# Root term formed at the head of the second edge loop, a middle stage written out by chunk, and the last additions' places read ahead

## The reference

```
h = max(layernorm(x), 0)
msg = relu(concat(h[src], h[dst], w) @ W1 + b1) @ W2 + b2
agg = segment_max(msg, dst)            (0 where a node has no edge)
x = x + relu(concat(h, agg) @ U1 + c1) @ U2 + c2
h = max(layernorm(x), 0)
W[r] = sum over b of w_comp[r, b] * weight[b]          (8 relations, 4 bases)
x = x + relu(h @ root_weight + segment_sum((h @ W[rel])[src], dst) + bias)
```

## Time and profile before

| | us |
|---|---|
| median of 3 runs (8218.98 to 8224.45) | 8222.21 |
| the profiled execution | 8227.52 |
| its span, to which all places below refer | 8225.5 |
| GpSimd busy | 5991.5 (73%) |
| TensorE busy | 5838.0 (71%) |
| VectorE busy | 4033.0 (49%) |
| ScalarE busy | 921.0 (11%) |

### The profile page before, as it was taken

The page is one execution under the profiler, slowest core; times in us unless marked ns, Lnnn a source line. Parts: engine busy times, 40 slices in busy tenths (PEclk is TensorE's granted clock), DMA queues, the critical chain, the costliest instruction groups (busy, mean ns, idle before and its releaser), DMA issues. The chain is left out here.

```text
span 8225.5 us, 99087 instructions
## 1 busy us (share of the span) xinstructions
PE 5838.0 (71%) x23786; PEld 4086.1 (50%) x23786; DVE 4033.0 (49%) x7231; ACT 921.0 (11%) x1415; POOL 5991.5 (73%) x6283
## 2 busy tenths in 40 slices
PE   6878878878778888888766666666666666666655
PEld 5555555555555555555544444444444444444444
DVE  5555555555555555555564444444444444444443
ACT  3111111111111111111130000000000000000001
POOL 4777777777777777777627777777777777777775
PEclk8998998899999888888887777777777777777777
DMA  6333333333333333333332222222222222222223
GB/s 183 99 99 97 97 99 97 97 98 98 97 97 99 97 97 97 99 97 97 86 85 53 53 53 53 53 53 53 53 53 53 53 53 53 53 53 53 53 53 68
DMA packets 452815, 644.74 MB, mean 78 GB/s; under 512 B 156658, under 2 KB 273082, under 8 KB 452260
## 3 DMA queue, kind: packets, MB, share of 16 engines
q0 software_dynamic: 200704, 411.44, 19.9%
q1 hardware_dynamic: 239284, 226.22, 9.9%
q10 hardware_dynamic: 12768, 6.42, 0.3%
HBM read 615.44 MB, written 28.13 MB: 78 GB/s over the span
## 5 line engine op out<-in xcount | busy, mean ns | idle before, releaser
L552 POOL DMA_INDIRECT G<-p_tab,idxs x3136 | 3031.2, 967 | 970.2 <-issue 950.6
L1106 POOL DMA_INDIRECT hT<-h_tab,idxs x3136 | 2959.0, 944 | 964.1 <-issue 953.6
L671 DVE TENSOR_TENSOR_SCAN R<-mk,R,psM 128x512 f32<-128x512 bf16 x784 | 1003.5, 1280 | 1576.2 <-PE psM L587 1537.2
L1124 PE MATMUL psA<-S,hT 128*128 128x256 f32 x3136 | 1142.4, 543 | 817.6 <-DMA hT<-h_tab,idxs 817.6
L1124 PE MATMUL psA<-hT 128*128 128x256 f32 x3136 | 945.3, 468 | 706.6 <-DMA hT<-h_tab,idxs 682.4
L1124 PEld LDWEIGHTS psA<-S,hT 128*128 128x128 f32 x3136 | 876.6, 286 | 1083.4 <-issue 885.6
L1124 PEld LDWEIGHTS psA<-hT 128*128 128x128 f32 x3136 | 737.3, 241 | 954.3 <-issue 751.9
L578 PE MATMUL psZ<-ident,G 128*128 128x128 f32 x3136 | 518.4, 289 | 731.9 <-DMA G<-p_tab,idxs 731.5
L587 PE MATMUL psM<-Z,w 128*128 128x512 f32 x1568 | 987.3, 717 | 0.0
L640 ACT ACTIVATE Z<-psZ,b1c 128x512 f32<-128x512 f32 x784 | 538.6, 687 | 3416.8 <-PE psZ L583 3414.0
L583 PE MATMUL psZ<-oh,Qw 65*128 65x512 f32 x1568 | 879.3, 644 | 11.9 <-DVE oh L661 11.9
(11 more groups left out here) (90 smaller groups left out, 3124.3 us busy)
## 6 DMA issues: line engine op xcount, KB each, us to landing
mk<-marks SPq DMA_DIRECT2D x392, 256.0 KB
G<-p_tab,idxs POOLq DMA_INDIRECT x3136
pl<-marks SPq DMA_DIRECT2D x392, 128.0 KB
hT<-h_tab,idxs POOLq DMA_INDIRECT x3136, 2.5
Qw<-q_tab SPq DMA_DIRECT2D x784, 32.0 KB
xa<-in_x SPq DMA_DIRECT2D x14, 448.0 KB, 5.1
p_tab<-pr SPq DMA_DIRECT2D x14, 448.0 KB, 3.3
oh<-in_w SPq DMA_DIRECT2D x392, 4.0 KB
```

Of the source, the lines that this page charges most:

```text
L552: pool.indirect_dma_start(G[:, r, j, :], None, p_tab, bass.IndirectOffsetOnAxis(ap=idxs[:, s, j:j + 1], axis=0)).then_inc(gathered[r], 16)
L671: nc.vector.tensor_tensor_scan(R[:, b, :], mk[:, r // 2, b * GE:(b + 1) * GE], psM[:, b, :], R[:, 1 - b, GE - 1:GE], ALU.add, ALU.max).the ...
L1106: pool.indirect_dma_start(G[:, s, j, :], None, h2_tab, bass.IndirectOffsetOnAxis(ap=idxs[:, s, j:j + 1], axis=0)).then_inc(l1_gathered[q], 16)
L1124: ins = nc.tensor.matmul(psA[:, b, u * NB * W:(u + 1) * NB * W], G[:, 2 * q + u, j, :], S[q // 2 % 2][:, q % 2, u * GT + j, :, :].rearrang ...
```

## The change

Five edits.

1. In the first loop's head the clearing of `aggT` is moved behind the one-hot tiles of groups 0 and 1 and the wait for the constants.
2. The middle stage has no loop any more; each chunk is written out. `x` comes by 14 transfers. GpSimd adds `c2` to `xa` chunk by chunk. The hidden layer is written over `hT`. The norm is that of the opening stage (`bn_stats`, `bn_aggr`, root, reciprocal, product, seven `Relu` activations with scale and bias). Its rows are written over the chunk of `aggT` that the first layer has read, and are stored from there. `psY` and `psX` are doubled.
3. The transposes, the root matmuls and their copies move to the head of the second loop, in a sequence of their own on TensorE and ScalarE ahead of everything else that these issue there; the rows are read from `aggT`, the result is written over them. The tiles are those of the loop (`A`, `psA`, `psV`). TensorE waits for `root_kept` of all chunks before the first sums, VectorE before its first addition. The weights and the bias are loaded by the first two transfers of this block.
4. The last 16 additions read their places in two batches of eight, ahead of the wait for `pair_done`.
5. Names, semaphores and tiles follow.

The core of the diff (the removed bodies of the middle stage stand above):

```diff
-                        if not again:
-                            nc.vector.memset(aggT[:, 0:NP + W], 0.0).then_inc(agg_zeroed, 1)
                         dve.wait_ge(place_ready, 1)
                         for s in range(HOT):
                             onehot(0, s)
                         dve.wait_ge(consts_loaded, 48)
                         if not again:
+                            nc.vector.memset(aggT[:, 0:NP + W], 0.0).then_inc(agg_zeroed, 1)
                             dve.wait_ge(agg_zeroed, 1)
...
+            def part(k):
+
+                return hT[:, k * CW:(k + 1) * CW]
+
+            def h2(k):
+
+                return aggT[:, k * CW:(k + 1) * CW].rearrange("p (t d) -> p t d", t=CH)
...
+                    for k in range(NCH):
+                        sp.wait_ge(normed2, k + 1)
+                        sp.dma_start(h2_rows[:, k * CH:(k + 1) * CH, :], h2(k)).then_inc(h2_stored, 16)
+                    sp.wait_ge(h2_stored, 16 * NCH)
...
+                    pool.wait_ge(wts_loaded, 16 * len(loads))
+                    for k in range(NCH):
+                        pool.wait_ge(x_again[k], 16)
+                        nc.gpsimd.tensor_tensor(rows(k), rows(k), c2b[:, :].unsqueeze(1).to_broadcast([P, CH, D]), ALU.add).then_inc(x_offset, 1)
...
                     def first_layer(k):
-                        after(pe, y1_relu, k)
+                        after(pe, y1_relu, k - 1)
...
                     def second_layer(k):
                         pe.wait_ge(y1_relu, k + 1)
-                        after(pe, x1_added, k)
+                        after(pe, x1_added, k - 1)
...
+                    for k in range(NCH + 1):
+                        if k < NCH:
+                            first_layer(k)
+                        if k >= 1:
+                            second_layer(k - 1)
...
+                        act.wait_ge(moments2_done, k + 1)
+                        nc.scalar.activation(std2[:, k % 2, :], mv2[:, k % 2, :, 1], ACT.Sqrt, bias=epsd[:, 0:1], scale=1.0).then_inc(std2_done, 1)
+
+                    def norm(k):
+
+                        act.wait_ge(scaled2, k + 1)
+                        for t in range(CH):
+                            ins = nc.scalar.activation(h2(k)[:, t, :], xa[:, k * CH + t, :], ACT.Relu,
+                                                       bias=nmr2[:, k % 2, t:t + 1], scale=rs2[:, k % 2, t:t + 1])
+                        ins.then_inc(normed2, 1)
+
+                    for k in range(NCH + 2):
+                        if k >= 2:
+                            deviation(k - 2)
+                        if k < NCH:
+                            update(k)
+                        if k >= 2:
+                            norm(k - 2)
...
+                    def take(k):
+                        dve.wait_ge(x_offset, k + 1)
                         dve.wait_ge(y2_done, k + 1)
+                        nc.vector.tensor_tensor(rows(k), psX[:, k % 2, 0:CW].rearrange("p (t d) -> p t d", t=CH), rows(k), ALU.add).then_inc(x1_added, 1)
+
+                    def moments(k):
                         dve.wait_ge(x1_added, k + 1)
+                        for t in range(CH):
+                            ins = nc.vector.bn_stats(stat2[:, k % 2, t, :], xa[:, k * CH + t, :])
+                        ins.then_inc(stats2_done, 1)
+                        dve.wait_ge(stats2_done, k + 1)
+                        for t in range(CH):
+                            ins = nc.vector.bn_aggr(mv2[:, k % 2, t, :], stat2[:, k % 2, t, :])
+                        ins.then_inc(moments2_done, 1)
...
+                    for k in range(NCH + 2):
+                        if 0 <= k - 2 < NCH:
+                            scale(k - 2)
+                        if 0 <= k - 1 < NCH:
+                            take(k - 1)
+                            moments(k - 1)
...
+                rooted = tag == ""
+                if rooted:
+                    rootw = sb("rootw", [P, D], fp32)
+                    biasc = sb("biasc", [P, 1], fp32)
+                    h2T = [A[:, c, :, :, :].rearrange("p b o w -> p (b o w)")[:, 0:CW] for c in range(2)]
+                    psH = [psA[:, 2 * c:2 * c + 2, :].rearrange("p b n -> p (b n)") for c in range(2)]
+                    psR = psV[:, :, :].rearrange("p c n -> p (c n)")
...
+                            def turn(k):
+                                after(pe, h2_kept, k - 1)
+                                for t in range(CH):
+                                    a = k * CW + t * P
+                                    ins = nc.tensor.transpose(psH[k % 2][:, t * P:(t + 1) * P], aggT[:, a:a + P], ident[:, :])
+                                ins.then_inc(h2_turned, 1)
+
+                            def root_term(k):
+                                pe.wait_ge(h2_kept, k + 1)
+                                after(pe, root_kept, k)
+                                for a, n in ((0, CA), (CA, CW - CA)):
+                                    ins = nc.tensor.matmul(psR[:, a:a + n], rootw[:, :], h2T[k % 2][:, a:a + n], start=True, stop=True)
+                                ins.then_inc(root_done, 1)
+
+                            turn(0)
+                            for k in range(NCH):
+                                if k + 1 < NCH:
+                                    turn(k + 1)
+                                root_term(k)
+                            pe.wait_ge(root_kept, NCH)
...
+                            def keep(k):
+                                act.wait_ge(h2_turned, k + 1)
+                                after(act, root_done, k - 1)
+                                nc.scalar.activation(h2T[k % 2], psH[k % 2][:, 0:CW], ACT.Copy).then_inc(h2_kept, 1)
+
+                            def keep_root(k):
+                                act.wait_ge(root_done, k + 1)
+                                nc.scalar.activation(aggT[:, k * CW:(k + 1) * CW], psR[:, 0:CW], ACT.Identity,
+                                                     bias=biasc[:, 0:1]).then_inc(root_kept, 1)
...
+                            if rooted and isinstance(k, int) and k == 0:
+                                dve.wait_ge(root_kept, NCH)
...
-                        for k in range(2 * (NPAIR - BEHIND), NGRP):
-                            if k // 8 == NOCT - 1:
-                                dve.wait_ge(pair_done, NPAIR + 1)
-                            add(k, min(k // 8, NOCT - 2), k)
+                        for k in range(2 * (NPAIR - BEHIND), 8 * (NOCT - 2)):
+                            add(k, k // 8, k)
+                        for o in (NOCT - 2, NOCT - 1):
+                            lasts = range(8 * o, 8 * o + 8)
+                            places = [dve.value_load(win[0:1, k:k + 1], min_val=0, max_val=NP) for k in lasts]
+                            dve.wait_ge(pair_done, NPAIR + (o == NOCT - 1))
+                            for k, r0 in zip(lasts, places):
+                                to = aggT[:, bass.ds(r0, W)]
+                                after(dve, l1_added, k)
+                                nc.vector.tensor_tensor(to, psV[:, k // 8 % 2, k % 8 * W:(k % 8 + 1) * W], to, ALU.add).then_inc(l1_added, 1)
```

More of the change, by code:

```diff
@@ L828, in gnn @@
             x1_added = sem("x1_added")
[L829 to L833, removed]
+            stats2_done = sem("stats2_done")
+            moments2_done = sem("moments2_done")
             std2_done = sem("std2_done")
             rs2_done = sem("rs2_done")
+            scaled2 = sem("scaled2")
             normed2 = sem("normed2")
[L837 to L842, removed]
-            loads = [(u1[:, 0, :], U1[0:D, :]), (u1[:, 1, :], U1[D:2 * D, :]), (u2[:, :], U2), (rootw[:, :], root),
-                     (c1c[:, :], col(c1)), (biasc[:, :], col(bias)), (c2b[:, :], c2.partition_broadcast(P))]
+            h2_stored = sem("h2_stored")
+            loads = [(u1[:, 0, :], U1[0:D, :]), (u1[:, 1, :], U1[D:2 * D, :]), (u2[:, :], U2),
+                     (c1c[:, :], col(c1)), (c2b[:, :], c2.partition_broadcast(P))]
             with nc.Block() as block:
@@ L876, in second_layer @@
                         pe.wait_ge(y1_relu, k + 1)
[L877 removed]
+                        after(pe, x1_added, k - 1)
                         for t in range(CH):
[L879 removed]
+                            ins = nc.tensor.matmul(psX[:, k % 2, t * P:(t + 1) * P], part(k)[:, t * P:(t + 1) * P], u2[:, :],
                                                    start=True, stop=True)
                         ins.then_inc(y2_done, 1)
[L883 to L910 removed]
+                    for k in range(NCH + 1):
[3 more added lines that the diff above has]
+                            second_layer(k - 1)
                 @block.scalar
@@ L946, in step @@
-                    def step(i, u):
-                        k = 2 * i + u
-                        update(k)
-                        if there(k - 1):
-                            square(k - 1, 1 - u)
-                        if there(k - 3):
```

(19 more changed lines are left out.)

139 lines of the change are left out of this document (39 added, 100 removed).

## The result

The changed kernel takes 8181.36 us (median of five runs, 8179.25 to 8182.69) beside 8222.21 for the kernel before (five runs, 8218.69 to 8224.45): ratio 0.995, interval 0.9939 to 0.996, 40.85 us or 0.5% less, and no two of the runs of the two kernels overlap. Its profiled execution took 8180.08 us, span 8178.3. The forecast was 8182.0.

The account below looks back on a forecast made before the run. Both loops were taken as bound by GpSimd's gather issue, about 1.25 us each, so only time outside could change: 3.0 - 34.2 + 0 - 9 = -40.2 from 8222.21, giving a median of 8182, range 8169 to 8204.

Parts of the forecast that it names:

- Memset, +3.0: First loop's head: the moved clearing takes 13.1 us and delays one-hot 2, costing 3.0 us, between 0.4 and 3.5.
- Middle stage, -34.2: Between the loops: TensorE stays the bound at 4.73 us a chunk; gathers start 34.2 us earlier, range -38 to -24.
- Root term, 0: Second loop's head: fourteen chunks at 3.1 us, 43 us in all, stay hidden behind GpSimd's first gathers; no time lost.
- the cover: Second loop's start: GpSimd may issue 64 gathers, 80 us, before it needs pair 0's sums, which hides the root work.
- Rival (d): Second loop's head: root phase outlasts GpSimd's 64 gathers above 5.4 us a chunk; at 8 us, 32 us lost, 8214; chance 0.02.
- Last additions, -9: Second loop's end: places read ahead in two batches shorten the sixteen additions; gain 5 to 10 us, taken as 9.
- (a): First loop's head: the memset holds the gathers, so the loss is 9.6 us and not 3.0, 8189; chance 0.07.
- (b): Middle stage: GpSimd's addition becomes the bound; at 6.5 us a chunk the gain is 12.7 for 34.2, 8204; chance 0.08.
- (c): Loop edges: each of 94 turns waits for code on GpSimd; slower from 0.43 us a turn, 8276 at 1 us; chance 0.04.

Follow-up runs that it names:

- the repeated run: The changed kernel itself, with nothing altered, run again on another chip beside the kernel before (9636.76 us): 9616.46 us, ratio 0.9978.

## Why the prediction was right

**What bounds it.** Right: both streams kept 965 and 944 ns a gather. GpSimd's waits other than "issue" in the second loop are 9.1 at the start and 2.4 in all.

**1. Memset, +3.0.** Measured 2.9 by the wait, 2.6 to 2.8 from the loop's first gather to the 41st. That the row begins late and the instruction lasts 13.1 us is borne out by the second place it stood in: 2.58 of "issue" and 10.56 again, and the next instruction held until 161.7. Every trace with the memset there has 2.57 or 2.58, every one with it at the old place 2.69. The Trainium skill (VectorE: DVE Perf Modes, "Zero memsets can be issued as uint32 (trn2)") gives one cycle per element, an estimated 13.1; by that, the trace agrees. I had put the end near 164; it came at 161.7, because the marks landed 3 us earlier than I had assumed and the whole profiled run was 2 us ahead there, 1.8 of them already at its first gather. The loss is unchanged, since GpSimd came as much earlier.

**2. Middle stage, -34.2.** Measured -35.4. The period is 4.57 and not 4.73: first layer 3.01, second layer 1.73, of which 1.56 to the next step's start. I added the second layer's full length instead of the time to its successor; 13 x 0.16 is 2.1 us. Chunk 0's first layer took 5.58 (4115.74 to 4121.32) for the assumed 4.75, which takes 0.8 back; together that is the 1.2 by which the stage beat the sum. GpSimd's addition, taken as 2.0, took 2.05. The Trainium skill (GPSIMD Engine Reference, section 3.1) had given the same estimate; by that, the trace agrees. The delay that I allowed for VectorE's small instruction beside GpSimd's additions shows at most once (1.92 us at 4129.95, 0.17 to 0.40 later), off the path. The loads that I let cancel did not quite: the stage starts 1.67 sooner after the last addition (12.22 for 13.89), and the first gather 0.42 later after the last norm (13.42 for 13.00).

**3. Root term, 0.** Right for this result: 2.93 a chunk for the 3.1 of the sum, 37.8 of the cover's 80 us used up. Its condition was narrower than I wrote. Rival (d), a root phase over 5.4 us a chunk, had a chance of 0.02 and 32 us as its price at 8 us a chunk; in the later runs it came, with 8.3 us a chunk and 35.1 us of waiting. The step that would have failed there is the claim that ScalarE and TensorE keep their own pace beside the gathers. I read it from a trace in which they do.

**4. Last additions, -9.** Measured -7.1, in the range of 5 to 10. Additions at 0.34 (I had 0.28 to 0.5), reads 4.88 (4.8). The mis-sized term is the gap: I let the second reads begin while the first burst was still running, but the 4.88 between the bursts are all eight reads.

**Sum.** 2.9 - 1.7 - 35.4 + 0.4 - 7.1 = -40.9, and the medians differ by 40.85. That it meets them to 0.1 us is luck, as runs of one kernel differ by 3 to 6 us. So is part of the nearness of -40.2: the additions gained 1.9 less than forecast, the middle stage 1.2 and its start and end 1.3 more. The profiled executions differ by 47.4; the other 6.6 lie in the opening (1.8 at the first gather) and inside the loops. There the first loop, from its first gather to its last addition, took 4019.3 us before and 4018.6 after, so the memset's loss is not to be seen at its end in this pair of traces: the rest of the loop was 3.3 us shorter, and the loop's gathers took 4.1 us less in all (3027.1 for 3031.2).

**The rivals.** (a) and (b) as told above. (c), a wait for code at the loops' edges, has no mark in the result: GpSimd's idle time is "issue" but for 22 us in the first loop and 12 in the second, mostly the starts. In the later runs both kernels are longer by 17 to 19%, so their length says nothing of where the changed program lies.

## What to carry to other kernels

Work hidden beside a stream is hidden only at the pace it keeps next to that stream: ask how much slower it may get before the cover ends (here 5.4 us a chunk by the forecast, an estimated 5.8 by the repeated run, (116.9 - 35.1) / 14, for the 2.93 that it takes), and try it held apart as one of the runs. Where a wait behind a stretch decides, starting the stretch earlier gains nothing, the wait grows by as much. Sum each step of a bound engine to the start of the next step, not to its own end, and don't take an idle time marked "issue" for one thing: ahead of the memset it was part of the instruction, ahead of the second burst of additions it was eight reads, ahead of ScalarE's copies neither. Other rows, or the same instruction at a second place, tell them apart.

## What the runs showed of the hardware that was not expected

The same program took 8222 us at first and 9629 to 9759 in all later runs, on four occasions. The stretches outside the loops kept their lengths (middle stage 75.92 and 75.26, last norm to first gather 13.42 and 13.41). Inside, a gather keeps its length and waits more. In 1000 to 2000 us of the changed kernel, GpSimd's gathers (groups by line; result first, repeated run second):

```profile
L552 POOL DMA_INDIRECT G<-p_tab,idxs x791 | 760.0, 961 | 241.1 <-issue 241.1
```

```profile
L552 POOL DMA_INDIRECT G<-p_tab,idxs x656 | 634.4, 967 | 367.1 <-issue 185.5 <-remote 135.6 <-PE psZ L583 45.7
```

791 gathers became 656. "remote" means that the profile shows a signal but no instruction that gave it. ScalarE stands idle for such signals for 646.8 of these 1000 us, and for none in the result. In the root term the delay could be set apart: there it is ScalarE whose instructions come late, and it is gone where no gather runs. In the second loop TensorE is late as well. Each run of sixteen sum matmuls (as the profile counts them) waits for its inputs only ahead of its first, and in the result the sixteen take 3.6 to 6.2 us together. In the repeated run, some 18 us after GpSimd had begun to issue again, they come one by one, 2.1 to 2.8 us apart (timeline, TensorE; the first line is from before that):

```profile
5139.83 7.07 PE L1101 MATMUL psA<-S,hT 128*128 128x256 f32 x32
...
5162.58 0.59 PE L1101 MATMUL psA<-S,hT 128*128 128x256 f32 x1 [2.21 <-issue]
5165.38 0.59 PE L1101 MATMUL psA<-S,hT 128*128 128x256 f32 x1 [2.21 <-issue]
```

So instructions are late there for which the program has no wait, and the signals between engines alone can't be the cause. Whether it is the fetching of code or something else inside or outside the core no run here tells, nor why the first runs were free of it.

The granted clock of TensorE followed its idle time: in the windows view 0.59 from 5040 to 5100, with TensorE busy 8.2 of the 60 us and its four root matmuls at 3.32, and 0.92 from 5116 to 5132, busy 13.3 of 16, with 1.74 for the same four: the rows of 1.2 and of 2.4 GHz.
